# Delta-rule attention on one core: another order for VectorE's solve steps, GpSimd's key work, the masked products and the gate's sigmoid

## The reference

```python
q = l2norm((x @ Wq)) / sqrt(K);  k = l2norm(x @ Wk);  v = x @ Wv;  gate = x @ Wg
g = cumsum(decay);  L = exp(g_i - g_j) below the diagonal
P = where(strict, (k * beta) @ k.T * L, 0)
Ainv = inverse of the triangular system of P
v = Ainv @ v;  k_cumdecay = Ainv @ (k_beta * exp(g))
for each chunk:                       # S is a 16 x 16 state per head
    attn = where(tril, q @ k.T * L, 0)
    v_new = v - k_cumdecay @ S
    o = q * exp(g) @ S + attn @ v_new
    S = S * exp(g_last) + (k * exp(g_last - g)).T @ v_new
o = rmsnorm(o) * norm_w * silu(gate);  out = o @ Wo
```

## Time and profile before

| What | Value |
|---|---|
| Median of three runs | 1225.05 us |
| The profiled execution | 1227.84 us, span 1225.6 us |
| Granted TensorE clock, mean | 0.928 of full |
| Busy: PE, PEld, DVE, ACT, POOL | 83%, 60%, 77%, 49%, 33% |
| DVE by fortieths of the span (tenths busy) | 3777736368999999999888897726887546899976 |
| The attention stage | about 228 to 765 us |

### The profile page before, as it was taken

How to read it: one execution, slowest core, us unless ns; L and a number is a source line. 1 busy time by engine, 2 the same in 40 slices (tenths; PEclk the granted TensorE clock), 3 DMA queues, 4 the chain that set the end, 5 groups by cost and what they waited for, 6 DMA issues and landing times. The chain is left out here.

```text
span 1225.6 us, 38519 instructions
## 1 busy us (share of the span) xinstructions
PE 1020.6 (83%) x15510; PEld 738.3 (60%) x15510; DVE 941.6 (77%) x2432; ACT 599.6 (49%) x1614; POOL 407.9 (33%) x580
## 2 busy tenths in 40 slices
PE   2999977876888887889878886679999886799968
PEld 2888863444555555556555665457888774255546
DVE  3777736368999999999888897726887546899976
ACT  2433336443677676777667665554433253200134
POOL 3666630311222212222222121224665448400037
PEclk9999988888999999999998987779999988899979
DMA  9000013244444444444444443200000023946003
GB/s 254 19 2 1 1 39 130 64 91 99 102 105 98 92 88 100 107 104 89 87 98 106 97 88 76 47 11 1 2 1 1 1 61 90 267 115 172 1 18 121
DMA packets 282625, 93.31 MB, mean 76 GB/s; under 512 B 208976, under 2 KB 275408, under 8 KB 282448
## 3 DMA queue, kind: packets, MB, share of 16 engines
q1 hardware_dynamic: 247056, 84.03, 28.6%
q10 hardware_dynamic: 35392, 6.82, 2.9%
HBM read 56.20 MB, written 30.41 MB: 71 GB/s over the span
## 5 line engine op out<-in xcount | busy, mean ns | idle before, releaser
L1772 DVE TENSOR_TENSOR delta_tmp<-delta_PR 128x130 f32<-128x130 f32 (+12 forms) x416 | 153.0, 368 | 9.4
L1769 DVE TENSOR_TENSOR delta_PR<-delta_PR,delta_tmp 128x130 f32<-128x130 f32 (+12 forms) x416 | 152.2, 366 | 9.3
L1422 PE MATMUL psum<-delta_T,delta_pad 128*32 128x128 f32 x2048 | 84.2, 333 | 33.0 <-DMA delta_T<-inverse_scratch 31.8
L1884 POOL TENSOR_TENSOR delta_S<-delta_E,delta_Bm 128x128 f32<-128x128 f32 x32 | 15.3, 477 | 285.2 <-issue 276.4
L1621 ACT ACTIVATE delta_y<-psum 32x128 f32<-32x128 f32 x256 | 68.7, 268 | 84.7 <-PE psum L1456 56.8
L1422 PEld LDWEIGHTS psum<-delta_T,delta_pad 128*32 128x32 f32 x2048 | 71.8, 134 | 42.8 <-DMA delta_T<-inverse_scratch 39.2
L506 POOL TENSOR_TENSOR ffn_H<-ffn_hid,ffn_H 128x512 fp32r<-128x512 f32 x48 | 61.8, 1292 | 57.6 <-DVE ffn_H L472 57.6
L1406 PE MATMUL psum<-delta_MV,delta_KT 32*32 32x128 f32 x2048 | 70.4, 291 | 11.7 <-ACT delta_E L1571 11.7
L1637 ACT ACTIVATE delta_wide<-delta_S 32x128 f32<-32x128 f32 x256 | 78.2, 305 | 3.2
L506 POOL TENSOR_TENSOR first_H<-first_hid,first_H 128x512 fp32r<-128x512 f32 x48 | 61.7, 1292 | 53.4 <-DVE first_H L472 53.4
L1406 PEld LDWEIGHTS psum<-delta_MV,delta_KT 32*32 32x32 f32 x2048 | 60.2, 114 | 22.8 <-ACT delta_E L1571 15.9
(11 more groups left out here) (278 smaller groups left out, 2586.6 us busy)
## 6 DMA issues: line engine op xcount, KB each, us to landing
within_scratch<-delta_PT SPq DMA_DIRECT2D x128, 64.0 KB, 1.9
delta_PR<-within_scratch SPq DMA_DIRECT2D x16, 512.0 KB, 4.6
inverse_scratch<-delta_PR SPq DMA_DIRECT2D x16, 512.0 KB, 3.0
space_T<-taps_scratch SPq DMA_DIRECT2D x8, 1024.0 KB, 5.9
X<-taps_scratch SPq DMA_DIRECT2D x8, 1024.0 KB, 8.8
X<-in_x SPq DMA_DIRECT2D x32, 128.0 KB, 10.0
turned_scratch<-gates_XT SPq DMA_DIRECT2D x16, 256.0 KB, 2.3
delta_xT<-turned_scratch SPq DMA_DIRECT2D x32, 128.0 KB, 3.8
```

Source lines behind the costliest of these rows:

```text
L1422: i = pe.matmul(bank[3][SUB * c:SUB * c + SUB, (2 * w + g) * P:(2 * w + g + 1) * P], M.pad[:, from_c:from_c + SUB], M.T[t % 2][:, h * P:(h ...
L1769: i = v.tensor_tensor(after, after, t3, ALU.add)
L1772: i = v.tensor_tensor(t3, column.to_broadcast([P, j, n_after]), row.to_broadcast([P, j, n_after]), ALU.mult)
```

## The change

SyncE issues keys_out and keys_in one slot later. ScalarE runs the second widen behind the gate's sigmoid and not ahead of keep_v. VectorE's list gets another order: own_heads and new_state of the first half stand together, then the additions to X of the tile before (add_o and new_stats, moved over the slot's end), sum_qk and faded_q, all ahead of the slot's first solve step; the 29 steps come in six groups instead of eleven; keep_within and keep_attn stand behind the last of them. GpSimd's middle_state waits for new_state (s_x) instead of own_heads (s_bm); fade_first moves from the head of the slot to behind gate_o of the slot before; and ahead of fade_first, decayed_k and kept_k GpSimd waits for the slot's score products (f_kk).

```diff
--- before.py
+++ after.py
@@ -1341,8 +1341,8 @@
     for n in range(SLOTS):
         at(rows_in, n + 1)
         at(decays_in, n)
-        at(keys_out, n - 1)
-        at(keys_in, n - 2)
+        at(keys_out, n - 2)
+        at(keys_in, n - 3)
         at(within_out, n - LAG_FORM)
         if n % 2 == 0:
             if 0 <= (n - 2) // 2 < NT // 2:
@@ -1663,9 +1663,9 @@
             inverse_in(a, B, M, S, n - LAG_APPLY, (2, 3), S.i_late)
         at(keep_y, Z, 1)
         at(root_qk, n)
-        at(widen, Z, 1)
         at(keep_v, n)
         at(sigmoid_g, n)
+        at(widen, Z, 1)
         at(exp_decays, n - LAG_FORM)
         at(keep_ot, n - LAG_OUT)
         at(keep_wt, n - LAG_APPLY)
@@ -1813,31 +1813,27 @@
     for n in range(SLOTS):
         Z, O = n - LAG_SCAN, n - LAG_OUT
         at(own_heads, Z, 0)
-        solve(n, 0, 1)
         at(new_state, Z, 0)
-        solve(n, 1, 3)
+        at(add_o, O - 1)
         at(sum_qk, n)
-        solve(n, 3, 6)
         at(faded_q, n - LAG_FORM)
-        solve(n, 6, 10)
+        if O - 1 < AHEAD * BLK:
+            at(new_stats, O - 1)
+        solve(n, 0, 7)
         at(scale_qk, n)
-        solve(n, 10, 11)
+        solve(n, 7, 9)
         at(own_heads, Z, 1)
-        solve(n, 11, 12)
+        solve(n, 9, 10)
         at(new_state, Z, 1)
-        solve(n, 12, 15)
+        solve(n, 10, 13)
         at(keep_gate, n)
-        solve(n, 15, 21)
+        solve(n, 13, 22)
         at(sum_o, Z)
-        solve(n, 21, 24)
+        solve(n, 22, 29)
         at(keep_within, n - LAG_FORM)
-        solve(n, 24, 25)
         at(keep_attn, n - LAG_FORM)
-        solve(n, 25, 29)
         at(scale_o, Z)
-        at(add_o, O)
-        if O < AHEAD * BLK:
-            at(new_stats, O)
+    add_o(NT - 1)
 
 
 def delta_gpsimd(g, own, B, M, S, run):
@@ -1878,7 +1874,7 @@
 
     def middle_state(t):
         g.wait_ge(S.s_e, 2 * t + 1)
-        g.wait_ge(S.s_bm, 2 * t + 1)
+        g.wait_ge(S.s_x, 2 * t + 1)
         if t > 0:
             g.wait_ge(S.s_wide, 2 * t)
         g.tensor_tensor(M.S1, M.E0, M.Bm, ALU.add).then_inc(S.s_1, 1)
@@ -1894,10 +1890,12 @@
 
     for n in range(SLOTS):
         Z = n - LAG_SCAN
-        at(fade_first, Z)
         at(middle_state, Z)
         at(fade_second, Z)
         at(gate_o, n - LAG_OUT)
+        if 0 < n <= NT:
+            g.wait_ge(S.f_kk, n)
+        at(fade_first, Z + 1)
         at(decayed_k, n)
         at(kept_k, n)
         if n in (SLOTS - 4, SLOTS - 3):
```

## The result

The changed kernel takes 1286.13 us (median of four runs, 1282.15 to 1290.93) against 1223.70 for the kernel before beside it: a ratio of 1.052, 95% interval 1.048 to 1.055. I had forecast 1256 us, slower by 2.5%, with a range that ended at 1277. The direction and the place were right, and the loss is twice the forecast of 31 us. The profiled execution has a span of 1288.8 us, 63.2 more than before.

A forecast was written before the change was run, and what follows sets the result against it. A loop of VectorE's work and a delay through SyncE, DMA and ScalarE bound the kernel; 1.4 + 1.8 - 1.0 + 0.2 = +2.4 us a pair over 13 pairs, +31 us, gave 1256 us, range 1233 to 1277.

The forecast's parts named there:

- The delay behind K: From the odd slot's keep_within start (K) through SyncE, a DMA and ScalarE to the next scale_qk: 9.6 us, staying.
- The even passage: From keep_within's start in an odd slot to that in the even slot: 9.6 us delay, then 10.5 from scale_qk.
- the single 0.13: On VectorE, each solve step directly behind another costs 0.13 us: 1.8 us a pair with new_state behind own_heads.
- the 1.9 that the prediction quotes beside it: By the page, an even slot's keys and fade_first would cost 1.9 us instead of 0.7, 16 us above forecast.
- TensorE in the odd slot: Even to odd keep_within start: tiles, apply, outputs and last steps take 16.2 us against VectorE's 15.6; 0.2 us added.
- rival D: Path of the inverse's tiles grows; apply and within take up to 1.7 us more: +4 a pair, 1277 us, chance 0.12.
- The keys beside PSUM reads: In odd slots GpSimd's keys run beside keep_within and keep_attn, costing about 0.1 us; contention saved 1.0 a pair.
- the loop: VectorE's work from even scale_qk to odd keep_within, plus the delay through SyncE, DMA and ScalarE: 33.3 us a pair.
- Slots outside the pairs: Slots ahead of and behind the 13 pairs of slots 7 to 31: nil, give or take 3 us.
- A: Rival: faster, the delay does not bind and VectorE's work alone counts: -2.4 us a pair, 1194 us, chance 0.08.
- B: Rival: it cancels, through quicker stores and keys missing solve steps in even slots: +0.5 a pair, 1231 us, chance 0.08.
- ScalarE's sigmoid ahead of widen: On ScalarE, the gate ready 1.5 us after scale_qk instead of 2.7: nil, 0.3 us a pair either way.

The follow-up runs named there:

- e1: The changed kernel with SyncE issuing pair_back ahead of within_out in odd slots: 1258.3 us, ratio 1.029.
- e8: The kernel before with the change's GpSimd part alone and the keys one slot later on SyncE: 1210.9 us, ratio 0.989.
- e5: The changed kernel with only keep_within and keep_attn taken back to behind solve step 24: 1233.7 us, ratio 1.010.
- e10: The kernel before with VectorE's new order alone, keep_within and keep_attn behind step 24: 1241.6 us, ratio 1.016.
- e6: The kernel before with only keep_within and keep_attn moved behind the 29th solve step: 1274.4 us, ratio 1.041.
- e3: The changed kernel with SyncE issuing pair_back ahead of within_out in odd slots and the inverse's tiles ahead of it in even ones: 1222.6 us, ratio 0.999.
- e7c: The changed kernel with 18 filler matmuls in front of apply's wait for its tiles in odd slots: 1271.8 us, ratio 1.041.
- e4: The kernel before with both of e3's SyncE orders: 1225.6 us, ratio 1.002.

## Why the prediction was right in kind and half the size

- *The delay behind K.* Taken at 9.6 us, measured 9.5; scale_qk was to wait 2 us or more, and waits 21.3 us in twelve slots, 1.8 in the mean, with 0.7 more at faded_q and 1.0 at the slot's first own_heads, which waits for TensorE. e1 shortened the delay and the time followed. Right.
- *The even passage.* 9.6 + 10.5 = 20.1 forecast, 19.9 measured. The terms in it (eight more steps, 0.13 us for each that stands behind another, key work stretching steps as before) sum to the right value. The counts hold in the traces (43 steps and 27 places before, 51 and 40 in the changed kernel), and so does the single 0.13, at 0.11 to 0.13 us over the sizes of step. The Trainium skill, VectorE: DVE Perf Modes, section The DRAIN you can't avoid, has the semaphore cost nothing extra. The rows disagree, with 0.44 us against 0.32. The keys and fade_first stretch the even slot's steps by some 0.5 us in the mean, near the 0.7 taken and far from the 1.9 that the prediction quotes beside it.
- *TensorE in the odd slot.* This step failed: apply's length was mis-sized. I summed 10.5 + 1.95 + 1.05 + 0.5 + 0.35 + 1.85 = 16.2 us and measured 18.6. The start of apply was right (10.64). Its length was taken from one row, 1.95 us, and is 3.47: +1.5 us a pair. Even in the kernel before seven of twelve odd slots had a longer one, mean 2.63, so the row was not typical; it comes from the shortest of the twelve odd passages (16.3 us, mean 17.1). There the longer applies were hidden: the passage takes 17.0 us in the mean with them and 17.2 without. And I let the wait in front of it grow from 1.9 to 4.4 us without asking what that does to TensorE's clock. In rival D I had the two extra 1.7 us but put them down to the late slots' clock, with 0.12.
- *The keys beside PSUM reads.* This term was mis-sized too. In odd slots I priced 0.1 us, with the products ending about at K. In fact they end 0.5 to 1.4 us ahead of K, with the last narrow steps still to come, and fade_first starts at once: the narrow steps take 0.46 us each where they took 0.27 before, +0.55 a pair. The groups of instructions over the twelve pairs (mean ns of one behind the comma), before and after:

```profile
L1758 DVE SCALAR_TENSOR_TENSOR delta_PR<-delta_PR 128x29 f32<-128x29 f32 (+1 forms) x36 | 19.3, 561 | 0.4
L1763 DVE SCALAR_TENSOR_TENSOR delta_PR<-delta_PR 128x29 f32<-128x29 f32 (+1 forms) x36 | 8.8, 273 | 0.9
```

```profile
L1763 DVE SCALAR_TENSOR_TENSOR delta_PR<-delta_PR 128x29 f32<-128x29 f32 (+1 forms) x37 | 16.0, 459 | 0.9
L1758 DVE SCALAR_TENSOR_TENSOR delta_PR<-delta_PR 128x29 f32<-128x29 f32 (+1 forms) x36 | 7.9, 248 | 0.8
```

  The order frees the narrow steps of even slots (561 to 248 ns), which lay beside the delay and cost nothing, and stretches those of odd slots (273 to 459), which lie on the loop.
- *Slots outside the pairs.* Taken as nil. Of the 63.2 us the twelve pairs from slot 7 on hold 52.7, the thirteenth (K of slot 5 to K of slot 7) 5.8, the end behind slot 31 0.9. The other 3.8 are there at K of slot 5 (291.51 against 287.70), while scale_qk of that slot is only 0.7 late: K lies later within the slot, and slot 5 has the first pair_back that waits behind it. No run takes this apart further.
- *Rivals.* A (faster, the delay does not bind) and B fell with scale_qk's wait. Its grain of truth is e8: GpSimd's part is worth 12 us where the order doesn't pay for it.
- *ScalarE's sigmoid ahead of widen* was priced at nothing and was not tried alone. From e5 (+11 us, with it and GpSimd's part) and e10 and e8 (+18 and -12, without) it is worth less than these can tell apart.

The forecast's 2.4, apply's 1.5 and the narrow steps' 0.55 come to 4.45 us a pair against 4.4 measured. That they meet so closely is in part luck, as the even passage is 0.2 under its forecast and apply's start 0.1 over.

## What to carry to other kernels

Before moving an instruction later on a busy engine, follow what other queues have in line behind it: keep_within's four stores stood ahead of two transfers that had nothing to do with it, and a move by five short steps cost 51 us in e6, while two calls moved in SyncE's list took the whole 62 us off the changed kernel in e3. Price an engine's work on the path by all its repetitions and by the idle time that will stand in front of it, not by one row. And work taken off an engine that has slack there gives nothing, as with the narrow steps of even slots: ask first on which side of the loop it lies.

## What the hardware showed that I had not expected

After TensorE had stood idle for 4.4 us the granted clock in apply's stretch was 0.57, near the lower of the two levels (1.2 GHz), and apply's 64 rows took 3.3 us instead of 1.95; with fillers in the wait the clock was 1.00 and they took 1.96. All twelve odd slots of the changed kernel had 2.9 us or more of idle time in front of apply, and a long apply. In the kernel before, with 1.1 to 2.4 us, it went either way: after 1.86 us of idle time apply took 1.95 us, after 1.81 us it took 3.28, at a granted clock of 0.57:

```profile
448.54 3.28 PE L1422 MATMUL psum<-delta_T,delta_pad 128*32 128x128 f32 x64 [1.81 <-DMA delta_T<-inverse_scratch]
```

So the gap just in front does not decide it alone. Idle 3.1 us in front of outputs and within went with a long within (3.59 us instead of 1.95, clock 0.52) in e4. The Trainium skill, TensorE: Matmul & The Clock Gate, section Part 1: The HAM clock gate, has the clock throttled by default and released by activity. The rows agree as far as they go, and the runs show its price on a path, 14 us by e7c.

A filler matmul on one column group took 0.22 us (two rows of 0.11), one of apply's, spread over four groups in turn, 0.06 (two rows of 0.03). And two VectorE instructions of the same size start 0.11 to 0.13 us further apart when the second needs the first one's result.
